# Layer norms: the variance as full-width products, its root and reciprocal on whole tiles

## The reference, cut to what matters

```
def _layernorm(x, axis=-1, eps=1e-05):
    m = jnp.mean(x, axis=axis, keepdims=True)
    v = jnp.var(x, axis=axis, keepdims=True)
    return (x - m) / jnp.sqrt(v + eps)

xn = _layernorm(x, axis=-1)
x = x + attention(xn, ...) + feed_forward(xn, ...)     # four times, with other weights and kinds
```

## Time and profile before

| what | value |
|---|---|
| median of 3 runs | 2058.14 us (2054.18 to 2058.67) |
| the profiled execution | 2054.93 us, of which the profile's span is 2053.1 us |
| mean granted clock of PE over the span | 0.955 of 2.4 GHz |
| n0 (first mean product to last multiplication) | 6.73 to 20.51 us |
| n1 | 356.58 to 368.47 us |
| n2 | 656.60 to 673.18 us |
| n3 | 806.70 to 823.28 us |

### The profile page before, as it was taken

How to read it: one execution, slowest core, us unless ns; L and a number is a source line. 1 busy time by engine, 2 the same in 40 slices (tenths; PEclk the granted TensorE clock), 3 DMA queues, 4 the chain that set the end, 5 groups by cost and what they waited for, 6 DMA issues and landing times.

```text
span 2053.1 us, 45861 instructions
## 1 busy us (share of the span) xinstructions
PE 1850.3 (90%) x16855; PEld 1191.3 (58%) x16855; DVE 1287.1 (63%) x2490; ACT 995.4 (48%) x2433; POOL 1072.0 (52%) x2252
## 2 busy tenths in 40 slices
PE   7799997867898885898999999999999999999987
PEld 5422664422244453445677777777777777677766
DVE  2544564685577422535777777777777777777753
ACT  2375232215321341434566656655665666566653
POOL 0521222323100302033888888887888878888873
PEclk7899999989999796899999999999999999999999
DMA  6044422200001333101222222222222222222221
GB/s 155 1 121 148 109 46 56 72 34 1 20 25 26 96 106 95 34 19 40 53 55 61 55 52 63 63 54 53 63 63 54 53 58 63 53 53 62 44 53 33
DMA packets 229260, 121.36 MB, mean 59 GB/s; under 512 B 141712, under 2 KB 208816, under 8 KB 228784
## 3 DMA queue, kind: packets, MB, share of 16 engines
q1 hardware_dynamic: 223424, 109.06, 21.3%
q0 software_dynamic: 5616, 9.38, 2.2%
HBM read 84.88 MB, written 36.68 MB: 59 GB/s over the span
## 4 chain that ended last, share of the span: by engine, by line
PE 22%; POOL 20%; issue 6%; SPq 3%; DVE 3%; DMA 3%; ACT 2%; POOLq 0%; DVEq 0%; ACTq 0%
POOL a_term L2594 8%; POOL a_z L2598 8%; PE ps L2046 5%; PE ps L2056 3%; PE ps L2245 3%; SPq L1979 2%; POOL a_rstd L2570 2%; POOL a_xnorm L2576 2%; DMA a_l<-a_v_dram 2%; PE ps L2276 2%; SPq L1987 1%; DVE a_v L2653 1%; PE ps L2212 1%; PE ps L2286 1%; PE ps L2221 1%
## 5 line engine op out<-in xcount | busy, mean ns | idle before, releaser
L2594 POOL TENSOR_TENSOR a_term<-a_z,a_l 32x14 f32<-32x14 f32 (+6 forms) x896 | 342.1, 382 | 70.3
L2598 POOL TENSOR_TENSOR a_z<-a_z,a_term 32x14 f32<-32x14 f32 (+6 forms) x896 | 341.7, 381 | 70.2
L2624 DVE SCALAR_TENSOR_TENSOR a_qkv<-a_raw,a_taps,a_qkv 128x1024 f32<-128x1024 f32 x192 | 247.0, 1286 | 6.1
L2046 PE MATMUL ps<-all_xn,a_w_qkv 128*128 128x512 f32 x512 | 246.9, 608 | 0.0
L388 POOL DMA_INDIRECT f_rows<-a_row,a_slots x32 | 35.7, 1116 | 192.1 <-DVE a_of_tile L377 146.7
L2245 PE MATMUL ps<-a_out_t,a_w_out 128*128 128x256 f32 x512 | 129.1, 395 | 1.9 <-ACT a_out_t L2468 1.7
L2046 PEld LDWEIGHTS ps<-all_xn,a_w_qkv 128*128 128x128 f32 x512 | 89.1, 193 | 69.3 <-issue 67.5
L2389 ACT ACTIVATE a_raw<-ps 128x512 f32<-128x512 f32 x128 | 76.3, 598 | 108.7 <-PE ps L2046 108.0
L2056 PE MATMUL ps<-a_w_z,all_xn 128*128 128x256 f32 x512 | 122.6, 383 | 0.0
L849 POOL DMA_INDIRECT f_sums<-a_y,a_xs x23 | 36.0, 1566 | 136.5 <-ACT a_y L798 133.5
L2588 POOL COPY a_z<-a_l 32x256 f32<-32x256 f32 x64 | 27.4, 429 | 152.3 <-DMA a_l<-a_v_dram 152.0
(11 more groups left out here) (331 smaller groups left out, 4303.7 us busy)
## 6 DMA issues: line engine op xcount, KB each, us to landing
a_gc_rows<-a_g_dram SPq DMA_DIRECT2D x64, 256.0 KB, 4.7
a_v_dram<-a_v SPq DMA_DIRECT2D x64, 256.0 KB
a_w<-in_f_w SPq DMA_DIRECT2D x24, 512.0 KB, 4.5
a_w_qkv<-in_a_w SPq DMA_DIRECT2D x16, 512.0 KB, 3.8
a_t_dram<-a_z SPq DMA_DIRECT2D x512, 8.0 KB
a_xs<-f_rows SPq DMA_DIRECT2D x46, 130.0 KB, 2.2
a_w_z<-in_a_w SPq DMA_DIRECT2D x16, 256.0 KB, 2.8
a_w_out<-in_a_wo SPq DMA_DIRECT2D x16, 256.0 KB, 3.1
```

The source lines that it names most:

```text
L2046: mm = pe.matmul(ps[:, to, :], w_qkv[:, k, mt * P:(mt + 1) * P], xn[:, k, b * T:(b + 1) * T], start=k == 0, stop=k == KC - 1)
L2594: pool.tensor_tensor(term[:, 0:j, j + 1:], z[:, 0:j, j:j + 1].broadcast_to([HP, j, n]), rows[:, j:j + 1, j + 1:].broadcast_to([HP, j, n]), ...
L2598: pool.tensor_tensor(z[:, 0:j, j + 1:], z[:, 0:j, j + 1:], term[:, 0:j, j + 1:], ALU.add).then_inc(sub_step, 1)
L2624: dve.scalar_tensor_tensor(to, rows, tap, to, ALU.mult, ALU.add).then_inc(conv_ready if j == TAPS - 1 else conv_step, 1)
```

## The change

The variance is now a product of full width, in the manner of the mean: `mean_of` is the stationary operand, the squares of a half are the moving one, 512 columns at a time, and the result is the variance of every token in every partition (two products for a half instead of eight). The root is taken over 128x512 instead of 128x4 and written to a whole tile `rstd` in SBUF, of which DVE takes the reciprocal over 128x512. The products that spread the reciprocals (L103) are gone, and the multiplications read `rstd` from SBUF instead of the spread copy in PSUM. DVE's list changes its order: reciprocal 0, the two multiplications of half 0, reciprocal 1, the two multiplications of half 1. Nothing else is changed in the program.

```diff
-        rstd = s.buf("rstd", [P, TT])
+        rstd = s.buf("rstd", [P, N])
...
                 for b in range(B):
                     pe.wait_ge(squared, KC * (b + 1))
-                    for tt in range(b * ST, (b + 1) * ST):
-                        for k in range(KC):
-                            mm = pe.matmul(ps[:, B + b, tt:tt + 1], square[:, k, tt * P:(tt + 1) * P],
-                                           mean_of[:, 0:1], start=k == 0, stop=k == KC - 1)
+                    for k in range(KC):
+                        mm = pe.matmul(ps[:, B + b, :], mean_of[:, :], square[:, k, b * T:(b + 1) * T],
+                                       start=k == 0, stop=k == KC - 1)
                     mm.then_inc(var_ready, 1)
-                for b in range(B):
-                    pe.wait_ge(rstd_ready, b + 1)
-                    for q in range(ST):
-                        tt = b * ST + q
-                        mm = pe.matmul(ps[:, 2 * B + b, q * P:(q + 1) * P],
-                                       rstd[:, tt:tt + 1].to_broadcast([P, P]), ident[:, :], start=True, stop=True)
-                    mm.then_inc(spread, 1)
...
                 for b in range(B):
-                    of = slice(b * ST, (b + 1) * ST)
+                    part = slice(b * T, (b + 1) * T)
                     dve.wait_ge(std_ready, b + 1)
-                    dve.reciprocal(rstd[:, of], rstd[:, of]).then_inc(rstd_ready, 1)
-                for b in range(B):
-                    dve.wait_ge(spread, b + 1)
+                    dve.reciprocal(rstd[:, part], rstd[:, part]).then_inc(rstd_ready, 1)
+                    dve.wait_ge(rstd_ready, b + 1)
                     dve.wait_ge(squared, KC * (b + 1))
                     for k in range(KC):
-                        part = slice(b * T, (b + 1) * T)
-                        dve.tensor_tensor(xn[:, k, part], xn[:, k, part], ps[:, 2 * B + b, :],
+                        dve.tensor_tensor(xn[:, k, part], xn[:, k, part], rstd[:, part],
                                           ALU.mult).then_inc(normed, 1)
...
                 for b in range(B):
-                    of = slice(b * ST, (b + 1) * ST)
+                    part = slice(b * T, (b + 1) * T)
                     act.wait_ge(var_ready, b + 1)
-                    act.activation(rstd[:, of], ps[:, B + b, of], ACT.Sqrt,
+                    act.activation(rstd[:, part], ps[:, B + b, :], ACT.Sqrt,
                                    bias=eps[:, 0:1]).then_inc(std_ready, 1)
```

More of the change, by code:

```diff
@@ L60, in sem, with layer_norm @@
         return self.sems[-1]
-def layer_norm(nc, name, ps, x, xn, mean_of, ident, ahead=None):
+def layer_norm(nc, name, ps, x, xn, mean_of, ahead=None):
     with Stage(nc, name) as s:
         square = s.buf("square", [P, KC, N])
-        rstd = s.buf("rstd", [P, TT])
+        rstd = s.buf("rstd", [P, N])
         eps = s.buf("eps", [P, 1])
         mean_ready, centred, squared = s.sem("mean_ready"), s.sem("centred"), s.sem("squared")
-        var_ready, std_ready, rstd_ready, spread, normed = (
-            s.sem("var_ready"), s.sem("std_ready"), s.sem("rstd_ready"), s.sem("spread"), s.sem("normed"))
+        var_ready, std_ready, rstd_ready, normed = (
+            s.sem("var_ready"), s.sem("std_ready"), s.sem("rstd_ready"), s.sem("normed"))
         eps_ready = s.sem("eps_ready")
-        ST = T // P
         with nc.Block() as block:
@@ L2996, in build @@
         if "n0" in stages:
-            layer_norm(nc, "n0", ps, x, xn, mean_of, ident)
+            layer_norm(nc, "n0", ps, x, xn, mean_of)
         if "a0" in stages:
@@ L3001, in norm @@
         def norm(name):
-            return lambda ahead: layer_norm(nc, name, ps, x, xn, mean_of, ident, ahead)
+            return lambda ahead: layer_norm(nc, name, ps, x, xn, mean_of, ahead)
         if "a1" in stages:
```

## The result

The changed kernel takes 2082.3 us (median of 4 runs, 2080.47 to 2086.8) against 2058.4 us before (2054.18 to 2063.72), a ratio of 1.0112 with a 95% interval from 1.0086 to 1.0138. It is slower, as forecast, by 23.9 us instead of 17 to 18; the median lies 0.3 us above the upper end of my range. The profiled execution took 2082.64 us, 27.7 more than that of before.

A forecast was written before the change was run, and what follows sets the result against it. Each norm was taken as bound by its own chain ending on DVE: four backs of 10.09 us, 40.4, less 22.5 before, give +17.9 us. Profiled 2054.93 gives 2072.8, the median 2076.0; 2075 was taken, range 2068 to 2082.

The forecast's parts named there:

- What bounds a norm: In each norm, its own chain: DVE's pair of multiplications ends it, and the next stage's PE starts 0.33 us later.
- The front costs nothing: Norm up to the root of half 0: two wide variance products take as long as eight narrow ones, set at 0.
- a root that moves: Sign of being wrong: the root of half 0 leaves its forecast distance from norm start (9.1, 7.3, 9.9, 10.0 us).
- rival 3: Wide variance product meets a slow clock in n2, n3: root slips about 1.6 us each; total +21, 2078; chance 0.09.
- The back, 10.09 us for a norm: Root, two reciprocals, two multiplication pairs and hand-overs after the change; four norms 40.4 us against 22.5 before.
- The root at 0.69: ACT's root over 128x512 in each norm, priced at 0.69 us from the pass of that form at L1166.
- The reciprocal from SBUF: DVE's reciprocal over 128x512 in each norm, twice, priced at 3.36 us by 6.3 ns a column.
- With the rest of the span as long as before: Expected sign in the profile after: a3 begins near 841.5 and the span behind it keeps its length.
- Rival 1: DVE's wide reciprocal from SBUF is cheap: at 0.69 us the norms gain 3.5 us, total 2055; chance 0.04.
- Rival 2: Wide variance products keep PE's clock high into the next stages, 11.8 us back, change costs 6: 2063; chance 0.05.
- My argument that 1.64 us of idling already makes it slow: Against rival 2: PE idles some 8 us or more ahead of the barrier, and is slow after 1.64 us already.

## Why the prediction was right or wrong

- **What bounds a norm**: right. DVE's last multiplication ends at 378.36 in n1, and a1 starts at 378.68, the same 0.32 us behind.
- **The front costs nothing**: right for the products. From the variance product's start to the table load n1 takes 2.06 us now (365.01 to 367.07) and took 2.02. In n2 the root came 8.90 us after the norm's start (682.92 - 674.02), forecast 9.9, because the mean products met the high clock sooner (5.22 us for eight records, 6.64 before). So one of my signs of being wrong, a root that moves, did occur, and to the side opposite of rival 3. That is most of why the norms hold 16.6 us and not 17.5; n0's root came 0.3 us later. Of n2 and n3 after:

```profile
674.02 5.22 PE L88 MATMUL ps<-all_x,all_mean_of 128*128 128x512 f32 x8 [5.03 <-PEq L1676]
...
682.92 1.27 ACT L129 ACTIVATE n_rstd<-ps,n_eps 128x512 f32<-128x512 f32 x2
...
834.57 1.88 PE L94 MATMUL ps<-n_square,all_mean_of 128*128 128x512 f32 x4
```

- **The back, 10.09 us for a norm**: measured 9.99 in each of the four (378.36 - 368.37 in n1). Four times that less 22.5 is 17.5, forecast 17.9. The root at 0.69 was right (0.686).
- **The reciprocal from SBUF**, the one price without a row of its form: 3.35 us, forecast 3.36. Taking the line through four rows of the same operation, and not the nearest operation of that size, was the right choice. The Trainium skill's repeat count of 8 (page "VectorE: DVE Perf Modes", section "First, the fixed hardware budget"), read as eight cycles an element, would have made it an estimate of 4.27 us; the trace disagrees.
- **"With the rest of the span as long as before"**: this step failed. It took the stages between the norms as shifted and otherwise unchanged, and put nothing in the sum for them. a1 with f1 grew by 7.5 us, and 16.6 + 7.5 = 24.1 is near the measured difference of 23.9. That the median still came within 0.3 us of my range is luck: its upper end was built from the highest run and from rival 3's 3 us, and not from this term. Rival 3 had the mechanism, a ramp of the clock at another place, but allowed it only 3 us, and only at a stage's first products. The runs showed it deep inside a1: same code, 287.7 or 295.4 us, by a shift of the start alone. I had rows for low clock at the start of stages, and didn't look at how sparse PE's work is behind them.
- **Rival 1** (a cheap reciprocal): excluded by 3.35 us. The kernel with the root's reciprocal on ACT, which has none on DVE at all, shows how far it could have gone at most: a back of 3.22 us a norm, slightly faster than before as a whole.
- **Rival 2**: the clock didn't pay anything back, since PE idles for 9.6 to 11.2 us ahead of each next stage. With PE filled it does in part. My argument that 1.64 us of idling already makes it slow was wrong: after 3.20 us of idling a1 starts at the high clock in the kernel with the root's reciprocal on ACT. In the kernel before, the clock had fallen earlier, while PE was still busy with the spreading products, as its row of n1 shows (PE busy for the whole us, clock 0.50):

```profile
366.00:367.00 1.00, 1.00 (x6) 0.86 (x5) 0.91 (x2) 0.00 (x0) 0.00 (x0) 0.50 0.28 82
```

  The Trainium skill's rule that the throttled state is the default and activity releases it (page "TensorE: Matmul & The Clock Gate", section "What's actually happening") agrees with a1's first four records: 3.75 us behind idling, 1.96 behind filling. It doesn't account for the falls while PE was busy.

What stays open: a2 and a3 differ by 1 to 3 us between the kernels in single profiles, and by 0.4 to 5 us between two profiles of the same kernel, so I can't say whether the change has a part in it. Nor is it known at which moments the clock can change; which start of a1 is a good one can only be tried.

## What to carry to other kernels

A reciprocal on the vector engine is priced by its columns, some five times a multiplication of the same size here; widening it from 4 columns to 512 to save products on an engine that has nothing else to do costs more than it frees. Where the price of an operation isn't in the trace, a line through the same operation at other sizes is better than another operation at the same size. And when a block ends in a barrier, look at what the matrix engine's clock does behind it: a delay of a few microseconds can cost or give back as much again in a later stage, and some products that nobody reads, beside the other engines' tail, bought 10 to 11 us in two versions of this kernel.

## What the runs showed of the hardware that I had not expected

- The time of a stretch of 288 us, which repeated to 0.12 us in each of the two kernels that were profiled twice, depends on when it starts: 287.7, 290.0, 287.4, 295.35 and 287.7 us for delays of 0, 2.1, 3.4, 5.5 and 6.8 us, with DVE, ACT and POOL busy for the same time to within 0.5 us, PE for 239.5 to 247.9 us, and its granted clock between 0.95 and 0.92. A kernel with 1.36 us more work in n1 took 7.5 us less for this stretch.
- PE's clock fell in microseconds in which PE was busy throughout: in the spreading products of n1 before (0.81 for 365 to 366, 0.50 for 366 to 367), and in the narrow products of a2 with PE filled (0.72 for 685 to 686). And it was high after 3.20 us without any product (start of a1 with the root's reciprocal on ACT).
- The vector engine's reciprocal from SBUF took 1.36 us for 193 columns, 3.35 for 512 and 5.45 for 848, 6.2 ns for each further column.
- The four records of two wide products took as long as the sixteen records of eight products of one column: 1.88 us (n3 after, above) against 1.84, both at the high clock.
